# A twelve-stage decoder on one core: the second half of each norm's mean goes to the stage ahead, and the last context attention is entered by its keys with its ternary rounding cut into pieces

## The chip, the cores and the metric

The kernel runs on one core of a Trainium2 chip, written by hand for its five engines: PE (TensorE, matmuls), DVE (VectorE), ACT (ScalarE), POOL (GpSimd) and SP (SyncE, which issues the DMAs). The metric is the device time of one execution in microseconds.

## What is computed

The reference is a decoder of four layers over x of shape (2, 512, 256), with a context of (2, 1024, 256). Each layer has a self part, a context part and a feed-forward part, each added to x behind a norm:

```python
x = x + _L3_attn_ref(_layernorm(x, axis=-1), ...)
x = x + _L3_xattn_ref(_layernorm(x, axis=-1), ctx_1024, ctx_1024, L3_xattn_Wq, L3_xattn_bq, ...)
x = x + _L3_ffn_ref(_layernorm(x, axis=-1), L3_ffn_W1, L3_ffn_b1, L3_ffn_W2, L3_ffn_b2)

def _layernorm(x, axis=-1, eps=1e-05):
    m = jnp.mean(x, axis=axis, keepdims=True)
    v = jnp.var(x, axis=axis, keepdims=True)
    return (x - m) / jnp.sqrt(v + eps)
```

The last context attention (`L3_xattn`) is causal over 512 of the context's positions, with 16 heads of 64. The last feed-forward rounds both weight matrices to -1, 0 or 1: each matrix is divided by the mean of its absolute values, rounded and clipped.

## The kernel before

Activations lie transposed: 256 features on two groups of 128 partitions, 1024 tokens along the free axis. The tokens are two halves of 512, one for each batch entry; they are called half 0 and half 1. The residual `k.X` stays in SBUF throughout.

The program is twelve stages (`STAGES`, one for each part of a layer), and each writes the order of its five engines out by hand. Between two stages stands a fence (`Kernel.fence`, L178): PE, DVE, ACT and POOL drain, and all five engines wait until the four have. In the profiled execution the fences lie at 206.9, 271.8, 365.8, 443.9, 600.6, 653.9, 995.6, 1360.2, 1397.3, 1546.3 and 1848.9 us.

Each stage begins with a norm (class `Norm`, from L183), and each half of it is a chain over three engines: PE makes the mean by a matmul with a matrix of 1/256 (`mean`, L201), DVE subtracts it (`centre`, L207), ACT squares (`square`, L214), PE makes the variance (`var`, L220), ACT makes the inverse root with a Ln and an Exp (`root`, L227 and L229), and DVE multiplies (`scale`, L237). `ln` is the stage's own norm, and `nxt` the norm of the stage behind it. A stage can do the first steps of `nxt` for half 0 as soon as half 0 of the residual is done (`resid(1)`): with `nxt.early = 1` it does mean, centre and square; with 2 also variance, root and scale. Before the change six of the eleven stages have 2, and the stages that end at 600.6, 653.9, 1360.2, 1397.3 and 1546.3 have 1 (five); the stage that ends at 653.9 keeps it. What is left is done behind the fence by `open_tensor`, `open_scalar` and `open_vector`; `open_tensor` always makes the mean of half 1 first, and with `early` at 1 it issues five bf16 matmuls on the identity (`beat`, L157), whose results nobody reads, ahead of the variance.

The last context attention is `l3_xattn` (L2818). Its weights come in eight groups of two heads, G = 8. A group has eight units, a unit being 128 queries of one half with its 128 to 512 keys; N = 64. One loop over `step` is written for each engine, so that at step s PE makes the scores of unit s (L2886), DVE adds the causal mask and takes the maxima of unit s-1 (L3010), ACT takes its exponentials (L2970), DVE takes the reciprocals of unit s-2 (L3023), POOL scales with them (L3074), PE transposes the probabilities of unit s-3 (L2896), which ACT and DVE copy out (L2990, L3049), and PE multiplies unit s-7 with the values (L2932). `CHUNKS` places the projections: for each group q, k and v of both halves, six chunks, each made by PE at a step `at` (L2916, v at L2911) in one PSUM bank, `p_bank`, and copied out by DVE (q at L3032, v at L3038) or ACT (k at L2980). Each chunk waits until the one ahead of it is out of the bank. The first four, q0, k0, q1, k1, are made at steps -6, -5, -4 and -3, and PE waits for all four ahead of unit 0.

At steps 6 and 14 DVE and POOL round one weight matrix each of the last feed-forward (class `Ternary`, L2782): DVE sums 2048 absolute values per partition (L2792), POOL sums over the partitions (L2806), DVE makes scale and inverse (L2794, L2796) and then scales, rounds and clips the 2048 columns in three operations (L2798, L2800, L2802), all of it at one place in DVE's program.

## Time and profile before

| | |
|---|---|
| median of 3 runs | 1893.58 us (1891.5 to 1898.21) |
| profiled execution, device time | 1895.19 us |
| its span, first to last instruction | 1893.9 us |
| mean granted clock of TensorE | 0.961 |
| busy: PE, DVE, ACT, POOL | 89%, 56%, 48%, 23% of the span |
| stage of the last context attention | 1546.3 to 1848.9 us, 302.6 us |
| last stage (feed-forward) | from 1848.9 us |

Times in the rows further down are microseconds from the start of the span. A row of a timeline is start, duration, engine, line, operation, what it writes and reads, shape and count; in brackets the time for which its engine sat idle just before it, and what ended that. `DVEq L178` there is a fence. A granted clock of 1.00 is 2.4 GHz, 0.50 is 1.2 GHz.

### The profile page before, as it was taken

To read this page: it belongs to the slowest core of one execution; us is meant where nothing else is said; L and a number is where in the kernel's file an instruction comes from. 1 tells how busy PE (TensorE), PEld (TensorE's weight loads), DVE (VectorE), ACT (ScalarE), POOL (GpSimd) and SP (SyncE) were. 2 spreads that over 40 slices of the span, in tenths; PEclk is the share of its full clock that TensorE was granted. 3 is DMA by queue.
4 is the path that set the end of the run, shared out by engine and by line. 5 is a ranking of instruction groups with operands and counts; after the bars stand their busy time and mean duration, and the time that the engine had idled before them with its cause. 6 is when DMAs were issued, how large, how long until landed. Compare 5 with 4: busy or idle time off the path is not lost. (4 is left out here: it accounts for less than half of the span.)

```text
span 1893.9 us, 23001 instructions
## 1 busy us (share of the span) xinstructions
PE 1680.7 (89%) x7780; PEld 862.7 (46%) x7780; DVE 1053.0 (56%) x2140; ACT 905.3 (48%) x1762; POOL 428.8 (23%) x536
## 2 busy tenths in 40 slices
PE   7899996888998679999887899999888987899997
PEld 3334444334665234344334555655434433445545
DVE  4631125483313659888925788888448614555525
ACT  2331214352333247777823778887433732455523
POOL 0000000000000244555401455555201101223310
PEclk9999998999999999999998899999998987899999
DMA  5000100001000000000107111010127110000000
GB/s 214 1 0 0 39 1 1 34 1 45 1 1 17 1 9 18 9 9 9 48 1 240 55 59 39 30 35 26 57 53 217 39 72 10 13 18 21 1 0 23
DMA packets 31844, 69.42 MB, mean 37 GB/s; under 512 B 4213, under 2 KB 18357, under 8 KB 30293
## 3 DMA queue, kind: packets, MB, share of 16 engines
q1 hardware_dynamic: 31728, 67.95, 11.0%
q8 instruction: 63, 1.03, 0.2%
q14 instruction: 53, 0.43, 0.1%
HBM read 55.78 MB, written 12.06 MB: 36 GB/s over the span
## 5 line engine op out<-in xcount | busy, mean ns | idle before, releaser
L2247 POOL TENSOR_TENSOR work<-work,arena_a 128x512 f32<-128x512 f32 x128 | 167.6, 1310 | 151.7 <-ACT work L2112 151.5
L1986 PE MATMUL ps<-identity,ctx_keys 128*128 128x128 f32 x1024 | 145.0, 281 | 17.1 <-ACT work L2112 14.5
L2201 DVE CUSTOM_DVE_ANT_0 ctx_keys<-ps,arena_b 128x1024 f32<-128x1024 f32 x128 | 154.9, 1212 | 7.2 <-ACT arena_b L2063 7.0
L1986 PEld LDWEIGHTS ps<-identity,ctx_keys 128*128 128x128 f32 x1024 | 118.6, 144 | 64.9 <-ACT work L2112 21.3
L2094 ACT ACTIVATE ctx_keys<-ctx_keys,small 128x1024 f32<-128x1024 f32 x128 | 146.8, 1147 | 0.7 <-DVE small L2201 0.7
L2213 DVE TENSOR_TENSOR work<-ps,arena_a 128x512 f32<-128x512 f32 x128 | 88.0, 688 | 42.6 <-PE ps L1986 37.9
L3074 POOL TENSOR_SCALAR ctx_keys<-ctx_keys,small 128x128 f32<-128x128 f32 (+3 forms) x128 | 66.4, 531 | 199.3 <-DVE small L3023 185.3
L2112 ACT ACTIVATE work<-ps 128x512 f32<-128x512 f32 x128 | 76.3, 596 | 60.1 <-PE ps L1986 56.7
L338 PE MATMUL ps<-work,arena_a 128*128 128x512 f32 x192 | 86.8, 605 | 7.9 <-DVE work L512 3.2
L1788 POOL TENSOR_SCALAR work<-work 128x1024 f32<-128x1024 int32 x64 | 66.5, 1040 | 112.7 <-DVE work L1741 112.2
L2970 ACT ACTIVATE ctx_keys<-ctx_keys,small 128x128 f32<-128x128 f32 (+3 forms) x128 | 70.7, 554 | 41.0 <-DVE small L3010 40.5
L157 PE MATMUL ps<-identity 128*128 128x512 bf16 x340 | 82.4, 391 | 7.4 <-ACT work L1427 3.0
L1588 PE MATMUL ps<-work 64*128 64x512 f32 x256 | 73.2, 648 | 16.7 <-DVE work L1741 14.5
L1975 PE MATMUL ps<-work 96*128 96x512 bf16 x256 | 78.3, 388 | 10.6 <-DMA work<-parts_k_L_xattn 5.8
L201 PE MATMUL ps<-resid,mean_matrix 128*128 128x512 f32 x96 | 55.4, 707 | 35.0 <-DVEq L178 20.9
L1741 DVE SCALAR_TENSOR_TENSOR work<-work,ps 128x1024 int32<-128x1024 f32 x64 | 78.0, 1218 | 12.2 <-ACT work L1679 12.1
L214 ACT ACTIVATE norm_parts<-normed 128x1024 f32<-128x1024 f32 x24 | 25.2, 1051 | 124.1 <-DVE normed L207 124.1
L1724 DVE TENSOR_SCALAR work<-work,small 128x512 int16<-128x512 f32 x128 | 81.0, 674 | 2.3
L1663 ACT ACTIVATE work<-work 128x512 f32<-128x512 f32 x128 | 80.3, 643 | 2.4 <-POOL work L1788 2.4
L3049 DVE COPY work<-ps 128x128 f32<-128x128 f32 (+1 forms) x64 | 31.4, 491 | 84.9 <-PE ps L2896 84.3
L1155 POOL PARTITION_ALL_REDUCE small<-small x4 | 1.4, 358 | 338.7 <-DVE small L1151 338.7
L1612 PE MATMUL ps<-arena_a,work 128*64 128x512 f32 x256 | 66.3, 622 | 1.6 <-DVE work L1759 1.5
(387 smaller groups left out, 3451.4 us busy)
## 6 DMA issues: line engine op xcount, KB each, us to landing
arena_b<-in_mask SPq DMA_DIRECT2D x2, 2048.0 KB, 8.9
arena_a<-in_groupT SPq DMA_DIRECT2D x2, 2048.0 KB, 14.9
head_weights<-in_w_L_xattn SPq DMA_DIRECT2D x8, 449.0 KB, 3.3
arena_a<-in_w_l_attn SPq DMA_DIRECT2D x1, 3072.0 KB, 14.5
head_weights<-in_w_L_attn SPq DMA_DIRECT2D x8, 384.0 KB, 3.0
work<-parts_q_L_attn SPq DMA_DIRECT2D x8, 384.0 KB, 4.5
work<-parts_k_L_attn SPq DMA_DIRECT2D x8, 384.0 KB, 5.3
work<-parts_k_L_xattn SPq DMA_DIRECT2D x15, 192.0 KB
```

The lines of the kernel that those rows point to most:

```text
L157: self.pe.matmul(bank, ib[:, 0:P], ib.unsqueeze(1).broadcast_to([P, 2, 2 * P]), start=True, stop=True)
L338: mm = pe.matmul(k.bank(i), wT[:, c, m * P:(m + 1) * P], src[:, c, :], start=c == 0, stop=c == DC - 1)
L1663: op = act.activation(ex[i % NE][:, h, :], ex[i % NE][:, h, :], ACT.Exp, scale=1.0 / FX, accum_out=sums[i % 4][:, h:h + 1])
L1724: op = dve.tensor_scalar(attn[i % 2][:, h * S:(h + 1) * S], ex[i % NE][:, h, :], recip[i % 4][:, h:h + 1], OFFSET - HALF, OP.mult, OP.add)
L1741: dve.scalar_tensor_tensor(out=score[i % NS], in0=sign[i % 2], scalar=-HALF, in1=s_bank[i % 2], op0=OP.mult, op1=OP.add).then_inc(*truncat ...
L1975: mm = pe.matmul(s_psum[i % NS][:, o:o + S], qs[h][0:ROWS, q0:q0 + P], ks[h][0:ROWS, b * keys + o:b * keys + o + S], start=True, stop=True)
L1986: mm = pe.transpose(t_psum[z][:, kt * P:(kt + 1) * P], prob[i % NP][:, o:o + P], k.iden[:, :])
L2094: act.activation(p, p, ACT.Exp, scale=-1.0, bias=minmax[:, i % 8:i % 8 + 1], accum_out=sums[:, i % 8:i % 8 + 1]).then_inc(*exped.up())
L2112: act.activation(PT[i // 4 % 2][:, 4:8, i % 4 * P:(i % 4 + 1) * P], t_psum[1].rearrange("p (k t) -> p k t", t=P), ACT.Copy).then_inc(*turn ...
L2201: dve.tensor_tensor_reduce(prob[i % NP], s_psum[i % NS], NEG[:, b, qt, :], -1.0, BIG * 3e8, OP.add, OP.min, minmax[:, i % 8:i % 8 + 1]).th ...
L2213: dve.tensor_tensor(PT[i // 4 % 2][:, 0:4, qt * P:(qt + 1) * P], t_psum[0].rearrange("p (k t) -> p k t", t=P), GT[:, b, 0:4, qt * P:(qt + ...
L2247: pool.tensor_tensor(p, p, GT[:, b, 4:8, qt * P:(qt + 1) * P], OP.mult).then_inc(*weighed_pool.up())
```

## The change

1. In all eleven stages with a norm behind them, `nxt.second = True`, and PE makes the mean of half 1 for it at the end of the stage, behind `resid(2)`; `open_tensor` leaves it out.
2. At the fences at 600.6, 1360.2, 1397.3 and 1546.3 `nxt.early` goes from 1 to 2.
3. The last context attention makes its first chunks in the order k0, q0, k1, v0 at steps -6 to -3, and q1, v1 at steps 0 and 1. Chunks 1 and 3 (q0 and v0) use the bank `t_bank[0]`, so that there are two banks for the first chunks, and unit 0 waits for half 0 of q and k alone.
4. `Ternary` is gone. DVE sums the weights' absolute values in eight pieces of 512 columns, one at each of steps 3 to 10; PE sums them over the partitions with one small matmul at step 15 into `p_bank`; DVE makes both scales at step 16; and the rounding is 24 operations on 512 columns, one at each of steps 17 to 40.
5. On the host, the query and key weights of the second layer's context attention are no longer put in another order of columns. No instruction changes by this.

The diff, cut to its core (item 1 stands in the same form in the other stages):

```diff
@@ class Norm
         if self.early < 1:
             self.mean(pe, 0)
-        self.mean(pe, 1)
+        if not self.second:
+            self.mean(pe, 1)
         if self.early < 2:
             self.var(pe, 0, beats=5)
@@ l2_ffn
-        nxt.early = 1
+        nxt.early, nxt.second = 2, True
...
         leave(pe, 1)
+        if nxt:
+            nxt.var(pe, 0)
+            nxt.mean(pe, 1, resid(2))
...
             nxt.square(act, 0)
+            nxt.root(act, 0)
...
         add(1)
+        if nxt:
+            nxt.scale(dve, 0)
@@ l3_xattn
-    CHUNKS = [(0, what, n, at) for what, n, at in (("q", 0, -6), ("k", 0, -5), ("q", 1, -4), ("k", 1, -3))]
+    CHUNKS = [(0, what, n, at) for what, n, at in (("k", 0, -6), ("q", 0, -5), ("k", 1, -4), ("v", 0, -3), ("q", 1, 0),
+                                                   ("v", 1, 1))]
...
+    chunk_bank = lambda x: t_bank[0] if x in (1, 3) else p_bank
...
-                if i % per == 0:
-                    pe.wait_ge(*q_out(2 * g + 2))
-                    pe.wait_ge(*k_out(2 * g + 2))
+                if i % nk == 0:
+                    pe.wait_ge(*q_out(2 * g + b + 1))
+                    pe.wait_ge(*k_out(2 * g + b + 1))
...
-                if x:
+                ps = chunk_bank(x)
+                if x >= 4:
                     pe.wait_ge(*chunk_out(x - 1))
+                if 2 <= x <= 4:
+                    pe.wait_ge(*chunk_out(x - 2))
+                if step == 2 * per:
+                    pe.wait_ge(*ternary(9))
...
             if step == -5:
                 ln.var(pe, 1)
+            if step == 2 * per - 1:
+                pe.wait_ge(*ternary(8))
+                pe.wait_ge(*chunk_out(x))
+                pe.matmul(p_bank[:, 0:8], k.one[:, :], am, start=True, stop=True).then_inc(*magnitude.up())
...
-            if step in (6, 14):
-                j = int(step == 14)
-                if j:
-                    dve.wait_ge(*tern[0].done(6))
-                dve.wait_ge(*ffn_in(1))
-                tern[j].vector(dve, w_ffn[j], k.tern[:, 2048 * j:2048 * (j + 1)], k.extra[:, 0:2048])
+            round_weights(dve, step)
...
+    def round_weights(dve, step):
+        if step == 3:
+            dve.wait_ge(*ffn_in(1))
+        if 3 <= step < 11:
+            p = step - 3
+            dve.tensor_reduce(am[:, p:p + 1], k.WB[:, 2560 + S * p:2560 + S * p + S], AX.X, OP.add,
+                              apply_absolute_value=True).then_inc(*ternary.up())
+        if step == 2 * per:
+            dve.wait_ge(*magnitude(1))
+            dve.tensor_reduce(scale, p_bank[:, 0:8].rearrange("p (j c) -> p j c", j=2), AX.X, OP.add).then_inc(*ternary.up())
+            dve.wait_ge(*ternary(9))
+            dve.tensor_scalar(scale, scale, D / (P * 2048), 1e-8, OP.mult, OP.max).then_inc(*ternary.up())
+            dve.wait_ge(*ternary(10))
+            dve.reciprocal(inv, scale).then_inc(*ternary.up())
+        x = step - 2 * per - 1
+        if 0 <= x < 24:
+            p, op = divmod(x, 3)
+            part, src = tmp[:, piece(p % 4)], k.WB[:, 2560 + S * p:2560 + S * p + S]
+            dve.wait_ge(*ternary(11 + x))
+            if op == 0:
+                dve.tensor_scalar(part, src, inv[:, p // 4:p // 4 + 1], ROUND, OP.mult, OP.add).then_inc(*ternary.up())
+            elif op == 1:
+                dve.tensor_scalar(part, part, ROUND, 1.0, OP.subtract, OP.min).then_inc(*ternary.up())
+            else:
+                dve.tensor_scalar(tern[:, piece(p)], part, -1.0, None, OP.max).then_inc(*ternary.up())
```

## Rows read from the trace of the kernel before

**Rows 1.** The page: busy us (share of the span) and instructions, by engine.
```profile
PE 1680.7 (89%) x7780; PEld 862.7 (46%) x7780; DVE 1053.0 (56%) x2140; ACT 905.3 (48%) x1762; POOL 428.8 (23%) x536
```

**Rows 2.** Windows: stretch, length, busy us by engine, granted clock, DMA share, GB/s.
```profile
1546.31:1577.66 31.35, 22.80 (x33) 7.93 (x34) 5.38 (x8) 4.95 (x7) 0.00 (x0) 0.66 0.28 109
...
1577.66:1646.89 69.23, 53.44 (x258) 28.07 (x258) 38.71 (x112) 27.19 (x82) 14.98 (x31) 0.87 0.05 14
...
1608.26:1611.94 3.68, 3.68 (x12) 1.52 (x13) 1.58 (x6) 1.80 (x5) 2.00 (x4) 0.50 0.02 4
...
1644.37:1649.50 5.13, 5.13 (x19) 2.96 (x20) 2.31 (x10) 2.24 (x7) 1.99 (x4) 0.50 0.01 2
...
1675.52:1730.43 54.91, 54.91 (x307) 28.98 (x305) 28.02 (x105) 29.86 (x88) 16.61 (x33) 1.00 0.06 18
```

**Rows 3.** Timeline, fences at 271.8, 365.8, 443.9: start, us, instruction, [idle before].
```profile
267.32 1.22 DVE L671 TENSOR_TENSOR resid<-ps,resid 128x1024 f32<-128x1024 f32 x1 [5.58 <-PE ps L643]
...
270.41 1.29 DVE L237 TENSOR_TENSOR normed<-normed,norm_parts 128x512 f32<-128x512 f32 x2 [1.87 <-ACT norm_parts L229]
...
271.81 1.98 PE L201 MATMUL ps<-resid,mean_matrix 128*128 128x512 f32 x4 [2.81 <-DVEq L178]
...
273.93 1.29 DVE L207 TENSOR_TENSOR normed<-resid,ps 128x512 f32<-128x512 f32 x2 [2.22 <-PE ps L201]
...
363.31 1.23 DVE L896 TENSOR_TENSOR resid<-resid,work 128x1024 f32<-128x1024 f32 x1 [0.77 <-ACT work L825]
...
365.88 3.63 PE L201 MATMUL ps<-resid,mean_matrix 128*128 128x512 f32 x4 [3.62 <-DVEq L178]
...
443.97 3.22 PE L201 MATMUL ps<-resid,mean_matrix 128*128 128x512 f32 x4 [2.82 <-DVEq L178]
```

**Rows 4.** Timeline, PE and DVE around the fences at 1360.2 and 1397.3.
```profile
1359.40 0.75 DVE L2228 SCALAR_TENSOR_TENSOR resid<-ps,vecs,resid 128x512 f32<-128x512 f32 x1 [0.97 <-PE ps L2042]
...
1367.97 1.96 PE L2290 MATMUL ps<-normed,arena_b 128*128 128x512 f32 x4 [2.94 <-DVE normed L237]
...
1405.04 3.67 PE L2514 MATMUL ps<-normed,extra 128*128 128x512 f32 x8 [2.94 <-DVE normed L237]
```

**Rows 5.** Timeline, ACT and DVE around the fences at 600.6 and 653.9.
```profile
598.23 1.05 ACT L214 ACTIVATE norm_parts<-normed 128x1024 f32<-128x1024 f32 x1
...
614.30 1.22 DVE L1439 TENSOR_REDUCE small<-normed 128x1 f32<-128x1024 f32 x1
...
652.80 1.06 ACT L214 ACTIVATE norm_parts<-normed 128x1024 f32<-128x1024 f32 x1 [22.32 <-DVE normed L207]
```

**Rows 6.** Timeline, PE at the entry of the last context attention.
```profile
1546.36 3.78 PE L201 MATMUL ps<-resid,mean_matrix 128*128 128x512 f32 x4 [0.89 <-DVEq L178]
...
1556.12 2.57 PE L2916 MATMUL ps<-normed,head_weights 128*128 128x512 f32 x4 [2.94 <-DVE normed L237]
...
1568.35 3.75 PE L2916 MATMUL ps<-normed,head_weights 128*128 128x512 f32 x4 [2.81 <-issue]
...
1577.66 0.80 PE L2886 MATMUL ps<-work 64*128 64x128 f32 x4 [0.87 <-ACT work L2980]
```

**Rows 7.** Timeline, the two ternary roundings: DVE, POOL and PE.
```profile
1596.72 2.28 DVE L2792 TENSOR_REDUCE small<-arena_b 128x1 f32<-128x2048 f32 x1
...
1607.49 1.62 POOL L3074 TENSOR_SCALAR ctx_keys<-ctx_keys,small 128x128 f32<-128x128 f32 x4 [7.03 <-issue]
...
1608.26 0.69 PE L2896 MATMUL ps<-identity,ctx_keys 128*128 128x128 f32 x2 [8.09 <-POOL ctx_keys L3074]
...
1644.37 0.69 PE L2896 MATMUL ps<-identity,ctx_keys 128*128 128x128 f32 x2 [6.95 <-POOL ctx_keys L3074]
```

**Rows 8.** Timeline, a 512-wide cast, and the tight unit (21) of the attention.
```profile
1861.94 0.43 DVE L3173 CAST parts<-arena_a 128x512 fp32r<-128x512 f32 x1 [0.63 <-ACT arena_a L3149]
...
1674.63 0.93 POOL L3074 TENSOR_SCALAR ctx_keys<-ctx_keys,small 128x256 f32<-128x256 f32 x2 [3.86 <-DVE small L3023]
...
1675.94 0.66 PE L2896 MATMUL ps<-identity,ctx_keys 128*128 128x128 f32 x4
```

More of the change, by code:

```diff
@@ L190, in __init__ @@
         self.w, self.b, self.put, self.spare = w, b, put, spare
-        self.shared, self.early = sq[0] is sq[1], 0
+        self.shared, self.early, self.second = sq[0] is sq[1], 0, False
         self.mean_done, self.var_done = k.signals("pe", 2)
@@ L315, in l0_attn @@
     if nxt:
-        nxt.early = 2
+        nxt.early, nxt.second = 2, True
     bank = lambda *i: [k.bank(j) for j in i]
@@ L610, in l0_xattn @@
     if nxt:
-        nxt.early = 2
+        nxt.early, nxt.second = 2, True
     scored, mixed = k.signals("pe", 2)
@@ L650, in tensor @@
                         nxt.var(pe, 0)
+                        nxt.mean(pe, 1, resid(2))
     def scalar(act):
@@ L713, in l0_ffn @@
     if nxt:
-        nxt.early = 2
+        nxt.early, nxt.second = 2, True
     l0_ffn_loads(k, k.sp)
@@ L779, in tensor @@
             nxt.var(pe, 0)
+            nxt.mean(pe, 1, resid(2))
     def mix(pe, h):
@@ L935, in l1_attn @@
     if nxt:
-        nxt.early = 2
+        nxt.early, nxt.second = 2, True
     l1_attn_loads(k, k.sp)
@@ L980, in tensor @@
             nxt.var(pe, 0)
+            nxt.mean(pe, 1, resid(2))
     def scalar(act):
@@ L1197, in l1_xattn @@
     if nxt:
-        nxt.early = 1
+        nxt.early, nxt.second = 2, True
     l1_xattn_loads(k, k.sp)
@@ L1272, in tensor @@
                 nxt.mean(pe, 0, resid(1))
+        if nxt:
+            nxt.var(pe, 0)
+            nxt.mean(pe, 1, resid(2))
     def scalar(act):
@@ L1351, in vector @@
         close(dve, 1)
+        if nxt:
+            nxt.scale(dve, 0)
     def close(dve, b):
@@ L1383, in l1_ffn @@
     if nxt:
-        nxt.early = 1
+        nxt.early, nxt.second = 1, True
     in_q, hid_q = Quantizer(k, view(k.small, 8, 4)), Quantizer(k, view(k.small, 12, 4))
@@ L1418, in tensor @@
             nxt.mean(pe, 0, resid(1))
+            nxt.mean(pe, 1, resid(2))
     def scalar(act):
@@ L1554, in l2_attn @@
     if nxt:
-        nxt.early = 2
+        nxt.early, nxt.second = 2, True
     l2_attn_loads(k, k.sp)
@@ L1651, in tensor @@
                         nxt.var(pe, 0)
+                        nxt.mean(pe, 1, resid(2))
     def scalar(act):
@@ L1872, in l2_xattn @@
     if nxt:
-        nxt.early = 1
+        nxt.early, nxt.second = 2, True
     thin_loads(k, k.sp, name)
@@ L2027, in tensor @@
         close(pe, 1)
+        if nxt:
+            nxt.var(pe, 0)
+            nxt.mean(pe, 1, resid(2))
     def turn_back(pe, n):
@@ L2118, in scalar @@
             nxt.square(act, 0)
+            nxt.root(act, 0)
     def gather(act, n):
@@ L2223, in vector @@
         absorb(dve, 1)
+        if nxt:
+            nxt.scale(dve, 0)
     def absorb(dve, n):
@@ L2276, in l2_ffn @@
     if nxt:
-        nxt.early = 1
+        nxt.early, nxt.second = 2, True
     l2_ffn_loads(k, k.sp)
@@ L2333, in tensor @@
         leave(pe, 1)
+        if nxt:
+            nxt.var(pe, 0)
+            nxt.mean(pe, 1, resid(2))
     def scalar(act):
@@ L2360, in scalar @@
             nxt.square(act, 0)
+            nxt.root(act, 0)
     def vector(dve):
@@ L2385, in vector @@
         add(1)
+        if nxt:
+            nxt.scale(dve, 0)
     sync(k.sp)
@@ L2443, in l3_attn @@
     if nxt:
-        nxt.early = 1
+        nxt.early, nxt.second = 2, True
     l3_attn_loads(k, k.sp)
@@ L2571, in tensor @@
             project(pe, m, (A_BANK[2], k.bank(3))[m], 1, (3,)).then_inc(*final.up())
+        if nxt:
+            nxt.var(pe, 0)
+            nxt.mean(pe, 1, resid(2))
     def transposed(pe, u, late):
@@ L2657, in scalar @@
             nxt.square(act, 0)
+            nxt.root(act, 0)
     def gather(act, v):
@@ L2731, in vector @@
         absorb(dve, 1)
+        if nxt:
+            nxt.scale(dve, 0)
     def finish(dve, x):
@@ L2827, in l3_xattn @@
     causal, wo, oT = view(k.WB, 0, S), view(k.WB, S, G, D), view(k.WA, 0, G, NT)
-    w_ffn = [k.WB[:, 2560 + 2048 * j:2560 + 2048 * (j + 1)] for j in range(2)]
     NP = 4
@@ L2840, in l3_xattn @@
     n_keys = lambda i: (i % nk + 1) * P
-    CHUNKS = [(0, what, n, at) for what, n, at in (("q", 0, -6), ("k", 0, -5), ("q", 1, -4), ("k", 1, -3))]
+    CHUNKS = [(0, what, n, at) for what, n, at in (("k", 0, -6), ("q", 0, -5), ("k", 1, -4), ("v", 0, -3), ("q", 1, 0),
+                                                   ("v", 1, 1))]
     for g in range(G):
-        CHUNKS += [(g, "v", n, per * g + n) for n in range(B)]
+        if g:
+            CHUNKS += [(g, "v", n, per * g + n) for n in range(B)]
         if g + 1 < G:
@@ L2851, in l3_xattn @@
     if nxt:
-        nxt.early = 2
+        nxt.early, nxt.second = 2, True
     l3_xattn_loads(k, k.sp)
     w_in = k.ahead["l3_xattn"]
-    tern = [Ternary(k, view(k.small, 200 + 4 * j, 4)) for j in range(2)]
+    tern, tmp, piece = k.tern, k.extra[:, 0:2048], lambda p: slice(S * p, S * p + S)
+    am, scale, inv = (view(k.small, o, n) for o, n in ((200, 8), (208, 2), (210, 2)))
     consts_in, ffn_in = k.signals("dma", 2)
-    part, scored, turn, pv, final = k.signals("pe", 5)
+    part, scored, turn, pv, final, magnitude = k.signals("pe", 6)
     k_out, exped, turned_0, gathered = k.signals("act", 4)
-    q_out, v_out, maxed, inverse, turned_1, resid = k.signals("dve", 6)
+    q_out, v_out, maxed, inverse, turned_1, resid, ternary = k.signals("dve", 7)
     (weighed,) = k.signals("pool", 1)
+    chunk_bank = lambda x: t_bank[0] if x in (1, 3) else p_bank
     chunk_out = lambda x: {"q": q_out, "k": k_out, "v": v_out}[CHUNKS[x][1]](2 * CHUNKS[x][0] + CHUNKS[x][2] + 1)
@@ L2915, in tensor @@
                     for c in range(DC):
-                        mm = pe.matmul(p_bank, W[g % 2][what == "k"][:, c, :], src[:, c, t0:t0 + S], start=c == 0,
+                        mm = pe.matmul(ps, W[g % 2][what == "k"][:, c, :], src[:, c, t0:t0 + S], start=c == 0,
                                        stop=c == 1)
@@ L2953, in close @@
                     nxt.var(pe, 0)
+                    nxt.mean(pe, 1, resid(2))
     def scalar(act):
@@ L2979, in scalar @@
                         act.wait_ge(*scored(per * (g - 1)))
-                    act.activation(kT[g % 2][:, half(n)], p_bank, ACT.Identity,
+                    act.activation(kT[g % 2][:, half(n)], chunk_bank(x), ACT.Identity,
                                    bias=weights[g % 2][:, 897:898]).then_inc(*k_out.up())
@@ L3031, in vector @@
                         dve.wait_ge(*scored(per * (g - 1)))
-                    dve.tensor_scalar(q[s][:, half(n)], p_bank, weights[s][:, 896:897], 0.125, OP.add,
+                    dve.tensor_scalar(q[s][:, half(n)], chunk_bank(x), weights[s][:, 896:897], 0.125, OP.add,
                                       OP.mult).then_inc(*q_out.up())
@@ L3066, in gpsimd @@
         for step in range(N + 2):
-            if step in (6, 14):
-                tern[int(step == 14)].gpsimd(pool)
             i = step - 2
@@ L3316, in lay_out @@
             ws, bs = list(ws), list(bs)
-            for j in range(2):
+            for j in range(2 if n == "L3_attn" else 0):
                 ws[j] = ws[j].reshape(D, DC, 8, 16).transpose(0, 1, 3, 2).reshape(D, D)
```

25 lines of the change are left out of this document (2 added, 23 removed).

## The prediction

> **What bounds the kernel now.** I read in this order. The page's busy times: TensorE (PE) is busy 89% of the span, the next engine 56% [rows 1]; so an edit is worth what it takes off PE's waits or off its time at half clock, and DVE, ACT and POOL matter where PE waits for them. Windows over the last context attention (1546 to 1849 us): from the fence to the first score PE has a granted clock of 0.66 and takes 31.35 us over 22.80 us of work; the next 16 units take 69.23 us at 0.87, while 16 units in the middle take 54.91 us, PE busy in all of it, at 1.00 [rows 2]. So this stage is PE-bound except at its entry and in its first 16 units. The timelines show why. Twice PE waits for POOL, 8.09 and 6.95 us, and behind each wait the clock is 0.50 [rows 2, 7]. At the entry the small groups of PE work alternate with DVE and ACT [rows 6]. Last the timelines at the other fences: behind every one PE makes the mean of half 1 first, 1.98 us at full and up to 3.78 us at half clock, and DVE's subtraction waits for it [rows 3, 6].
>
> **Part 1, the mean of half 1 ahead of the fence (11 fences).** It needs the second residual half, so it can't come earlier than that plus its own time. What it gains depends on what else sets the fence.
>
> Where DVE scales half 0 behind the residual, the scaling covers it. At 271.8 the residual ends at 268.54 and the scaling (1.29 us) starts only at 270.41 [rows 3]; PE sits idle for the last 2.81 us before the fence, from 269.0, so mean 1 runs to 271.0 and the fence stays. PE's first work then moves from 273.7 to 271.85, DVE's subtraction from 273.93 to 271.85: gain 2.1. Three more are of this kind. At 443.9 the same cover holds and the mean removed cost 3.22 us, partly at half clock [rows 3]: 3.3. At 365.8 it cost 3.63 [rows 3], but the residual ends only 1.3 us before the fence, so 2 us of mean move the fence by 0.7, by 2.4 if they fall at half clock: gain between 1.2 and 2.9, 2.2 taken. At 995.6 the residual is as late: the fence moves by 0.7, PE gains 2.0 behind it, and the stage goes on with transfers through memory that start 0.7 later (SP's mask and group loads stand behind the fence too): -0.7 to +1.3, I take 0.7. At 1848.9 it is hidden, but nothing waits for it behind the fence, since DVE splits half 0 first: 0. At 206.9 no scaling is left behind the residual, mean 1 only changes sides: -0.1. At 653.9 the fence is set by ACT's square, which ends at 653.86 [rows 5], and mean 1 ends at 653.2: the fence stays and what follows comes 1.8 earlier.
>
> **Part 2, early 1 to 2 (behind four fences).** Variance 0, its root and the scaling of half 0 go ahead of the fence, and five filler matmuls go. At 1360.2: PE ends its projection at 1359.4, where DVE's last residual starts [rows 4], variance 0 to 1361.2, root 0.69 + 0.63, scaling 1.29 (row of the same kind in [rows 3]): fence at 1364.0 in place of 1360.2, mean 1 hidden under the root. L2290 starts there, at 1364.05 in place of 1367.97 [rows 4]. Half 1 gains a little less, since its variance now stands directly behind L2290: 3.4. The next fence (1397.3) has the same order, but variance 0 and mean 1 overlap ACT and residual better: L2514 from 1405.04 [rows 4] to 1401.3, 3.7; SP's three loads and POOL's memsets start 4 us later there, and their first reader is later still. At 600.6: square 0 ends at 599.3 [rows 5], so the fence is at 604.0; subtraction, square, variance, root, scaling of half 1 lead to the second maximum at 611.2 in place of 614.30 [rows 5]: 3.1 at full clock, 1.4 if the variance falls at half clock because its fillers are gone; 2.0 taken. Sum of the ten fences: 2.1 + 3.3 + 2.2 + 0.7 + 0 - 0.1 + 1.8 + 3.4 + 3.7 + 2.0 = 19.1 us, between 9 and 24.
>
> **Part 3, the entry of the last context attention.** Now: fence 1546.3, mean 3.78, fillers, variance, root, scaling, q0 at 1556.12, wait, k0 1559.62, variance 1, wait for the scaling, q1 1568.35, wait, k1 1573.04, wait, first score 1577.66 [rows 6]. After: the last projection ends 0.89 us before PE's mean [rows 6], at 1545.4, variance 0 takes 1.9 to 3.6, root 1.4, scaling 1.3: fence between 1550.0 and 1552.5, I take 1551. Then k0, q0, variance 1, k1, v0 need nothing that PE has to wait for: k0 no norm at all, q0 half 0, and two banks take turns, so an eviction (0.75 us) runs under the next chunk. Variance 1 needs subtraction and square, ready 2.4 us behind the fence; PE gets to it after 3.7. Five groups of 1.88 to 1.98 us are 9.5 us at full clock, at half (3.75 us per chunk [rows 6]) 17. Since PE is then dense from that projection on, but for about a microsecond before the fence, I take full clock but for 1 us: first score at 1561.5, gain 16.1; bounds 8 and 18. The chunk q1 moves behind the first score and takes the place there that v0 had: no cost. The causal mask must land before unit 0 and the weights before the first sum; both were issued behind the fence and need 3 and 10 us, under the 10 us of chunks and the steps that follow.
>
> **Part 4, the ternary rounding.** Removed, twice: a sum of 2048 (2.28 us), POOL's sum over partitions (0.40), two small operations and three of 2048 (1.29 + 1.23 + 1.23) in one piece on DVE, while TTR and reciprocals of the attention queue behind it. POOL comes back to its scalings only 7.03 us after that sum [rows 7], longer than DVE's part explains. PE's waits are 8.09 + 6.95 = 15.0 us; the half clock behind them (3.68 and 5.13 us at 0.50 [rows 2]) costs half of 8.8, 4.4. Together 19.4. Added: eight sums of 512 on DVE in steps 3 to 10, 24 operations of 512 in steps 17 to 40 (0.43 us each, by the row of a 512-wide cast [rows 8]; the sums by a quarter of 2.28, 0.57), one tiny matmul in step 15, and in step 16 a wait of PE's v chunk for DVE's sum over its result. Behind that wait stand PE's mix of that step and the next score; DVE does the sum right behind unit 15's maxima, near the time PE gets there: at most 0.5. The pieces stand on DVE between the maxima and the reciprocal, so a unit's scaling on POOL comes 0.43 later. Seven of eight units have 2 to 5 us between POOL's end and PE's transposes; the tight one is every eighth: POOL ends at 1675.57, PE starts 1675.94 [rows 8], slack 0.38. Three or four such units lose 0.1 to 0.5 each. Taken off: 1.0. Net 18.4, between 12 (clock gains nothing, every piece shows a little) and 19.4.
>
> A piece on DVE with one SBUF source may also hold up POOL. The rows don't decide it: POOL's next scaling starts at 1607.49 [rows 7], behind DVE's three large operations, where it lacked its reciprocal anyway. The Trainium skill ("SBUF — State Buffer", "SBUF: two separate sides") says more: such a DVE operation and a GpSimd operation take a shared port pair for a whole instruction, and the other fully blocks. By it each piece could add another 0.43 us to POOL's part; beside the sum above that would be some 2 us more.
>
> **Sum.** 19.1 + 16.1 + 18.4 = 53.6 us. Against the profiled execution's 1895.2 us: 1841.6; the median of the runs is 1.6 lower, which gives 1840. I forecast 1841.
>
> **Rivals.**
> (a) *Half clock stays at the places made dense.* For: clock 0.66 over the entry now [rows 2], and the fillers are gone behind four fences. Against: waits of 2.8 us before a mean left it at 1.98 us [rows 3]. Entry gain 8 to 10, fences 3 to 5 less: about 1853. The Trainium skill ("TensorE: Matmul & The Clock Gate", "Part 1: The HAM clock gate (the "warmup" mystery)") says that throttled is the default and that sustained matmul activity releases it. By that rule the dense entry would end at full clock, nearer to my forecast.
> (b) *The mean only changes sides.* If every fence moves by what is saved behind it, as at 206.9, the 19.1 fall away: 1860. Against: the cover at 271.8 and 653.9 is in the rows [rows 3, 5].
> (c) *The pieces show.* If each of the 32 pieces holds PE for 0.43 to 0.86 us, 14 to 27 us of the rounding's gain come back: about 1861. Against: slack of 2 to 5 us in seven of eight units.
> (d) *Slower than before.* Place: units 17 to 40, where the 24 pieces stand. If waits for late transposes break up PE's work so often that it runs at half clock, a unit of 54.91 / 16 = 3.43 us takes 6.9. It decides from 16 such units on (16 x 3.43 = 55 us, more than the sum); all 24 give 1841 + 82 = 1923. Against: 1.00 and no gap now, and a piece of an eighth of a unit.
> (e) *More than the sum.* Waits that I put at one place also ended at others, and the clock gains in stages that I count as shifted only: 1829.
> That the change doesn't do what it says (some other transfer or bank holds the entry) is a case of (a) by price.
>
> **How the numbers follow.** Forecast (1832 to 1848) 0.66, (a) 0.14, (b) 0.05, (c) 0.06, (d) 0.02, (e) 0.07. The range takes forecast and (a), 1832 to 1855. A difference of 0.3% (5.7 us) is about what can be told from none. All but (d) and a small rest lie beyond it on the fast side: faster 0.96, within 0.3% 0.02, slower 0.02.
>
> **What would show it.** Part 1 and 2: behind each fence no L201 on PE, DVE's subtraction at once, and the fence-to-fence lengths shorter by the terms above. Part 3: five groups without a gap and a first score 10 to 12 us behind the fence. Part 4: no PE wait over 1 us in units 5 to 16, 16 units from the first score in some 50 us, and period 27.5 us per eight units unchanged. It is wrong if PE's busy time in units 17 to 40 has gaps, if the granted clock at the entry stays near 0.5, or if stage lengths elsewhere stay as they are.

## The result and the profile after

The changed kernel takes 1847.3 us (median of 4 runs, 1846.75 to 1848.24), the kernel before beside it 1892.54 us (4 runs). The ratio is 0.9758, with a 95% interval from 0.9734 to 0.9781. The forecast was 1841 with a range of 1832 to 1855: the sign and the range hold, and the sum of the gains was 6 us too large. The profiled execution took 1846.75 us (span 1845.4), 48.4 us less than that of before.

The page of the changed kernel, busy times by engine; PE is busy 21.9 us less than in [rows 1]:

```profile
PE 1658.8 (90%) x7762; PEld 854.0 (46%) x7762; DVE 1052.5 (57%) x2163; ACT 905.1 (49%) x1762; POOL 428.8 (23%) x534
```

Windows of the changed kernel (columns as in [rows 2]): from the fence to the first score, 16 units, 16 units with rounding pieces in them, and the whole stage of the last context attention, from fence to fence:

```profile
1539.97:1548.87 8.90, 8.84 (x32) 4.90 (x32) 3.33 (x5) 3.63 (x5) 0.00 (x0) 1.00 0.88 353
1548.87:1599.88 51.01, 49.06 (x250) 24.88 (x249) 30.90 (x107) 26.06 (x80) 14.12 (x28) 1.00 0.08 24
1599.88:1654.85 54.97, 54.97 (x306) 28.97 (x304) 32.95 (x121) 29.73 (x88) 16.46 (x32) 1.00 0.06 18
1539.97:1800.78 260.81, 255.81 (x1298) 132.01 (x1298) 132.64 (x463) 124.25 (x358) 66.85 (x128) 1.00 0.07 25
```

The entry fell from 31.35 to 8.90 us, the next 16 units from 69.23 to 51.01, all at full clock, and 16 units with 15 of the 24 rounding pieces among them take 54.97 us with PE busy throughout, where 16 quiet ones took 54.91 [rows 2]. Over the whole stage the clock is 1.00. The timeline of PE at that entry (columns as in [rows 6]):

```profile
1535.33 1.88 PE L220 MATMUL ps<-norm_parts,mean_matrix 128*128 128x512 f32 x4
1537.05 1.88 PE L201 MATMUL ps<-resid,mean_matrix 128*128 128x512 f32 x4
1540.03 1.98 PE L2929 MATMUL ps<-ctx_feat,head_weights 128*128 128x512 f32 x4 [1.10 <-DVEq L178]
1541.85 1.88 PE L2929 MATMUL ps<-normed,head_weights 128*128 128x512 f32 x4
1543.57 1.88 PE L220 MATMUL ps<-norm_parts,mean_matrix 128*128 128x512 f32 x4
1545.28 1.88 PE L2929 MATMUL ps<-ctx_feat,head_weights 128*128 128x512 f32 x4
1547.00 1.95 PE L2924 MATMUL ps<-head_weights,ctx_feat 128*128 128x128 f32 x16
1548.88 0.49 PE L2894 MATMUL ps<-work 64*128 64x128 f32 x4
```

Variance 0 and mean 1 stand ahead of the fence; behind it come k0, q0, variance 1, k1 and v0 without a gap.

Where the 48.4 us are: 41.8 in the stage of the last context attention (302.56 to 260.81, fence to fence), 6.3 in the ten stages ahead of it, 0.3 in the last. The forecast had 39.2 in that stage and 14.4 ahead of it: its 53.6, where the later fence (4.7 us at 1546.3) counts against the ten stages and for the entry.

### The profile page after: what moved, and what is told of

It is laid out like the page before. It is cut to its first block and busy times, and to the rows that moved or that the text cites. A ratio compares the mean times of both kernels' runs of the same rounds, so it can differ in the third digit from the quotient of the medians.

```text
span 1845.4 us, 22986 instructions
## 1 busy us (share of the span) xinstructions
PE 1658.8 (90%) x7762; PEld 854.0 (46%) x7762; DVE 1052.5 (57%) x2163; ACT 905.1 (49%) x1762; POOL 428.8 (23%) x534
## 5 line engine op out<-in xcount | busy, mean ns | idle before, releaser
L1989 PE MATMUL ps<-work 96*128 96x512 bf16 x256 | 79.3, 393 | 14.2 <-DMA work<-parts_k_L_xattn 9.4
L1647 PE MATMUL ps<-normed,head_weights 128*128 128x512 f32 x128 | 63.7, 620 | 3.8 <-DVE work L1746 3.0
## 6 DMA issues: line engine op xcount, KB each, us to landing
arena_a<-in_groupT SPq DMA_DIRECT2D x2, 2048.0 KB, 14.8
```

The costliest lines, as they stand in the source:

```text
L1989: mm = pe.matmul(s_psum[i % NS][:, o:o + S], qs[h][0:ROWS, q0:q0 + P], ks[h][0:ROWS, b * keys + o:b * keys + o + S], start=True, stop=True)
```

## The experiments

All times are medians; "before" is the kernel before, run on the same chip alongside (1892.98 to 1896.05 us there).

**One half of the change at a time.** `norm_moves_only` has items 1 and 2 of the change and leaves items 3 and 4 out.

> All eleven norm moves (the mean of half 1 at every fence, the variance at four), with the last context attention's chunks and its rounding as before. Theory S (the sum as forecast): the ten other fences give 19.1 us, and at the fence of 1546.3 mean, fillers, variance, root and scaling (about 8 us) leave the entry, of which the order q0, k0, q1, k1 keeps its waits: 27 us faster than before. Theory T (transfers started by the fence set the pace of the second layer's and the last layer's attention, so the gains at 995.6, 1397.3 and part of 653.9 are given back there): the ten fences give 9, and the whole 15 to 18 us. Under T the gain counted up to the fence of 1546.3 is 8 to 10 us, under S 19.

Measured: 1876.58 us (1872.96 to 1877.35), before 1892.98; ratio 0.9896 (0.9860 to 0.9931). That is 16.4 us, T's value and not S's 27, though the interval reaches from 13 to 27. S's 27 was also added up wrongly: it takes the 8 us off the entry in full, while the forecast itself has 4.7 of such work come back ahead of the fence at 1546.3, which leaves 22. T's size doesn't prove T's places: by the means in the table further down, 0.4 us are given back behind 653.9, 0.6 behind 995.6 and 3.4 behind 1397.3. In this profile the first score comes 16.71 us behind the fence, with q1 at half clock (3.48 us).

`last_attention_only` has items 3 and 4 and leaves the norms as they were.

> Only the last context attention is changed (keys first, two banks, rounding in pieces); all norms as before. Stages ahead of it keep their lengths within 1 us. Forecast: rounding 18.4 us, and from the entry what the order of the chunks gives without the earlier variance, about 8: 26 us faster. Theory T with norm_moves_only: the gains of the two kernels add up to the 45.3 us of the whole change within 3 us. Rival C (the clock makes the two help each other, since half 1's chunks come at full clock only if the norm's gap is gone too): the two add up to less than 42.

Measured: 1862.19 us (1858.31 to 1869.78), 30.8 less than before; ratio 0.9832 (0.9784 to 0.9881). More than the forecast's 26. 16.4 and 30.8 make 47.2, and the whole change gave 45.2 on one chip and 49.6 on another: they add up, and nothing speaks for C.

`pieces_only` has item 4 alone.

> Only the ternary rounding is cut into pieces; norms and the order of the first chunks as before. Forecast: 18.4 us faster than before (12 to 19.4), no PE wait over 1 us in units 5 to 16, the entry as long as before. Rival (the rounding's gain as read in the changed kernel was partly the entry's, by its clock): 12 us or less.

Measured: 1871.73 us (1864.33 to 1880.3, 7 runs), before 1896.05; ratio 0.9890 (0.9853 to 0.9928), 14 to 28 us. The rival's 12 us or less is out. PE has no wait over 0.8 us behind the first score, and from there to the last fence of the stage it takes 251.3 us, against 271.2 before. But the entry, whose code is that of before, took 25.27 us and not 31.35, at a granted clock of 0.90 and not 0.66. That was expected by neither theory.

`keys_first_only` has item 3 alone; of its edit, the order of the chunks:

```diff
-    CHUNKS = ... (("q", 0, -6), ("k", 0, -5), ("q", 1, -4), ("k", 1, -3))
+    CHUNKS = ... (("k", 0, -6), ("q", 0, -5), ("k", 1, -4), ("v", 0, -3), ("q", 1, 0), ("v", 1, 1))
```

> The kernel before with only the order of the first chunks and the second bank; norms and rounding as before. The norm chain behind the fence stays, and k0 runs under it. Forecast from the rows of before: q1 (3.75 us), k1's wait and two evictions leave the path to the first score, some 8 to 12 us; the two waits of the roundings (15.0 us) stay. last_attention_only was 30.8 us faster than before and pieces_only 20 to 24, which also leaves 7 to 11 for this part. Rival (the second bank helps only when the norm is there already): 4 us or less.

Measured: 1885.83 us (10 runs), before 1894.12; ratio 0.9945 (0.9923 to 0.9967), 6 to 15 us. The first score comes 14.88 us behind the fence, and PE's two waits at the roundings are there (7.75 and 7.34 us). The median's 8.3 us is at the low end of the forecast's 8 to 12, and the rival's 4 or less is out. With `pieces_only` it makes 32.6 us by medians, against 30.8.

**Is the half clock at the old entry the rule?** `before_again` and `after_again` are the two kernels unchanged, for second profiles.

> The kernel before once more, for a second profile of it. In pieces_only, whose entry to the last context attention is that of the kernel before, the first score came 25.27 us behind the fence at full clock, not 31.35 as in the profile that the forecast read. Theory V (the half clock at that entry comes and goes from one execution to the next, and the profiled execution had all of it): this profile shows the first score at 25 to 28 us, a stage of 296 to 300 us in place of 302.6, and the roundings' two waits unchanged. Rival (the entry at half clock is the rule, and pieces_only was the exception): 31 us and 302 us again. Ratio of times 1.

Measured: 1894.36 us, ratio 1.0027 (0.9999 to 1.0056). Windows of this second profile of before (fence to first score, next 16 units), and its timeline at the entry:

```profile
1548.93:1574.20 25.27, 16.73 (x33) 6.16 (x34) 5.37 (x8) 4.95 (x7) 0.00 (x0) 0.90 0.34 136
1574.20:1642.02 67.82, 52.72 (x259) 27.46 (x259) 38.70 (x112) 27.20 (x82) 14.99 (x31) 0.88 0.05 14
```

```profile
1548.98 3.78 PE L201 MATMUL ps<-resid,mean_matrix 128*128 128x512 f32 x4 [0.89 <-DVEq L178]
...
1559.11 1.96 PE L2916 MATMUL ps<-normed,head_weights 128*128 128x512 f32 x4 [2.94 <-DVE normed L237]
...
1568.48 1.96 PE L2916 MATMUL ps<-normed,head_weights 128*128 128x512 f32 x4 [2.81 <-issue]
...
1574.20 0.49 PE L2886 MATMUL ps<-work 64*128 64x128 f32 x4 [0.87 <-ACT work L2980]
```

The waits are those of [rows 6] (2.94, 2.81, 0.87), but q1 takes 1.96 us and not 3.75. The stage takes 295.75 us instead of 302.56. V holds: the 6 us of half clock at that entry come and go between executions (of three profiles with this entry, one has 31.35 us and two have 25.27), while the two rounding waits stay (7.83 and 6.52 us). The shorter entry is not at full clock throughout, as V's text has it of `pieces_only`: the mean ahead of it still takes 3.78 us, and the granted clock is 0.90. What decides between the two isn't shown.

> The changed kernel once more, on the same chip as before_again. First score 8.90 us behind the fence and a stage of 260.8 us again; the nine stages ahead of it add up to 1540 to 1543 us (1539.97 in its first profile). Theory V: the difference of the two kernels' times stays 45 us; that of the stage of the last context attention is 36 to 39 us by these two profiles, not 41.8 as by the first two.

Measured: 1844.74 us (1843.96 to 1850.62), before 1894.25; ratio 0.9757 (0.9712 to 0.9803). The first score again at 8.90 us and the stage at 260.80; the ten stages ahead took 1537.67 us, a little under the span expected. By the two new profiles the stage gained 34.95 us, just under V's 36 to 39, and the stages ahead of it 11.3. The medians on this chip differ by 49.5 us, not by 45.

**What of the rounding costs?** `rounding_in_two_bursts` is the changed kernel, with the 24 operations made six:

```diff
-        x = step - 2 * per - 1
-        if 0 <= x < 24:
-            p, op = divmod(x, 3)
...
+        if step in (2 * per + 1, 3 * per + 1):
+            j = int(step == 3 * per + 1)
+            src, dst = k.WB[:, 2560 + 2048 * j:4608 + 2048 * j], tern[:, 2048 * j:2048 * (j + 1)]
...
```

> The changed kernel, but the 24 rounding operations of 512 columns are six of 2048, three in a row at step 17 and three at step 25; sums and PE's sum over partitions stay in pieces. Forecast's reading of the waits removed (DVE's three long operations in one piece, 3.75 us, hold the maxima and reciprocals of the units behind them): each burst holds PE for 3 to 5 us, 6 to 10 us slower than the changed kernel, with PE waiting for POOL's scaling twice. Rival (the waits before came from POOL's own sum over the partitions, after which POOL came back only 7.0 us later): within 2 us of the changed kernel.

Measured: 1850.14 us (1848.72 to 1851.75), before 1894.12, ratio 0.9764 (0.9732 to 0.9796); the stage takes 264.18 us instead of 260.8. Timeline of this kernel, DVE, POOL and PE at the first burst:

```profile
1602.29 1.28 DVE L3091 TENSOR_SCALAR extra<-arena_b,small 128x2048 f32<-128x2048 f32 x1
...
1603.61 1.23 DVE L3093 TENSOR_SCALAR extra<-extra 128x2048 f32<-128x2048 f32 x1
...
1604.87 1.23 DVE L3095 TENSOR_SCALAR ternary_weights<-extra 128x2048 fp32r<-128x2048 f32 x1
...
1606.01 0.16 DVE L3036 RECIPROCAL small<-small 128x2 f32<-128x2 f32 x1
...
1606.26 1.36 POOL L3111 TENSOR_SCALAR ctx_keys<-ctx_keys,small 128x512 f32<-128x512 f32 x2 [3.78 <-DVE small L3036]
...
1606.90 2.02 PE L2924 MATMUL ps<-head_weights,ctx_feat 128*128 128x128 f32 x16 [1.60 <-DVE work L3051]
```

The same three long operations that stood ahead of the 8.09 us wait in [rows 7] now cost PE 1.60 us, and 1.39 at the second burst, not for POOL but for a copy of DVE. So cutting the three long operations is worth 3.4 us, by the stage, of the 18.6 to 19.3 that the whole rounding gave; the medians (1850.14 against 1844.74 to 1849.85 for the changed kernel and near relatives) can't tell so little. Both texts were off in size: the forecast's reading (6 to 10) by more than the rival's. The other 15 us or so hang on what is common to this kernel and the changed one: POOL's sum over partitions gone to PE, DVE's sum of 2048 cut and moved ahead, and the operations at steps 17 and 25 instead of 6 and 14. These were not separated by a run. The rows of before allow an estimate for the first wait of 8.09 us. DVE is held there from 1596.72 [rows 7] to 1604.61, 7.89 us, of which 1.49 is its own wait for POOL's sum; that is 4.2 more than the 3.72 of the burst, which cost PE 1.60. And POOL starts its scaling 2.7 us after the reciprocal that it needs (1604.77 to 1607.49), where in the burst it starts 0.1 after it. If PE pays for both in full, 1.6 + 4.2 + 2.7 make 8.5, near the 8.09:

```profile
1600.49 0.15 DVE L2794 TENSOR_SCALAR small<-small 128x1 f32<-128x1 f32 x1 [1.49 <-POOL small L2806]
...
1604.61 0.16 DVE L3023 RECIPROCAL small<-small 128x2 f32<-128x2 f32 x1
```

**Where the fences' gain goes.** `one_variance_undone` is the changed kernel with the variance of half 0 taken back at one fence, 1397.3 (stage `l2_ffn`):

```diff
-        nxt.early, nxt.second = 2, True
+        nxt.early, nxt.second = 1, True
...
-            nxt.var(pe, 0)
...
-            nxt.root(act, 0)
...
-            nxt.scale(dve, 0)
```

> The changed kernel with the variance, root and scaling of half 0 back behind the fence at 1397.3 (early 1, five filler matmuls again; the mean of half 1 stays ahead). Forecast: 3.7 less 1.9 for the mean that stays, so 1.8 to 2 us slower than the changed kernel. Theory T (all that the earlier fence gave is taken back by the transfers of the last layer's attention): within 1 us of it, or up to 2 us faster, since the three loads then have time to land ahead of the stores.

Measured: 1848.02 us (1840.98 to 1850.83) against 1847.3, 1848.28 and 1844.74 for the changed kernel and near relatives on three chips: the time doesn't decide. The profile shows more, by DVE's position in the stage behind, `l3_attn`, counted from the fence ahead of `l2_ffn`. There DVE comes to a place where it waits for PE's next score. Its last instruction ahead of that wait starts at 84.59 us, against 78.85 in the changed kernel: the earlier variance brings 5.7 us there. The first behind it starts at 86.70 against 85.61: 1.1 are left. In the kernel before the two start at 89.22 and 90.33, so against it 10.4 us become 4.7. The wait, in the changed kernel and with the variance taken back:

```profile
1442.23 0.42 DVE L2748 CUSTOM_DVE_ANT_0 arena_b<-ps,arena_b 128x256 f32<-128x256 f32 x1 [6.69 <-PE ps L2560]
```

```profile
1439.79 0.42 DVE L2744 CUSTOM_DVE_ANT_0 arena_b<-ps,arena_b 128x256 f32<-128x256 f32 x1 [2.04 <-PE ps L2556]
```

What is left at the fence that ends `l3_attn` can't be read so finely: it comes at 186.6 us, and with the variance in place, the code of these two stages being the same, at 182.8 to 185.8 in six profiles. T is right on the place; whether it is right on "all" stays open. The timeline of SP shows what lies between. First the changed kernel, its fence at 1390.98:

```profile
1391.01 0.32 SPq L2488 DMA_DIRECT2D work<-in_alibi_q  x1
1391.37 0.35 SPq L2489 DMA_DIRECT2D work<-in_alibi_k  x1
1391.77 0.27 SPq L2490 DMA_DIRECT2D work<-in_alibi_one  x1
1397.49 1.59 SPq L2497 DMA_DIRECT2D parts_q_L_attn<-arena_a  x3
...
1408.55 0.33 SPq L2521 DMA_DIRECT2D work<-parts_q_L_attn  x1
```

Then the kernel before, its fence at 1397.27:

```profile
1397.30 0.32 SPq L2462 DMA_DIRECT2D work<-in_alibi_q  x1
...
1411.45 1.59 SPq L2471 DMA_DIRECT2D parts_q_L_attn<-arena_a  x3
...
1419.17 0.33 SPq L2495 DMA_DIRECT2D work<-parts_q_L_attn  x1
```

The first stores are issued 6.5 us behind the fence and not 14.2, but their read-back, which waits for them to land, only 11.06 us after them and not 7.72. In the changed kernel the stores run into the three loads that the fence starts. With the variance taken back the distance is 7.83 again (1399.71 to 1407.54). That is 3.3 of the 7.7 us by which the stores are earlier. More goes in the later round trips of the same kind: the fourth read-back is issued 38.8 us behind the fence where it was 42.0, only 3.1 us earlier. The reader sees the end of it on PE, in the changed kernel:

```profile
1440.84 0.93 PE L2614 MATMUL ps<-work 111*128 111x512 bf16 x2 [6.36 <-DMA work<-small]
```

`alibi_later` moves these loads:

```diff
     def sync(sp):
-        sp.dma_start(qs[0:BIAS], a["alibi_q"].bitcast(BF16)).then_inc(*const_in.up())
...
+            if x == 1:
+                sp.dma_start(qs[0:BIAS], a["alibi_q"].bitcast(BF16)).then_inc(*const_in.up())
...
```

> The changed kernel with one edit: in the last layer's attention SP issues its three loads of the position table (alibi) behind the first two stores of the cut-up activations, not ahead of them. In the changed kernel the first of these stores lands 4.7 us after its issue (2.6 before), and PE waits 6.4 us for the pieces that come back. Theory T (that queue sets the pace, and the loads stand in front of it): the wait shrinks to what it was before the change and the kernel is 2 to 5 us faster than the changed one. Forecast's reading (the loads cost nothing there): within 1 us of it.

Measured: 1851.65 us (1849.69 to 1854.66), not faster. The transfers that T named do hold up the first round trip, for the distance from store to read-back falls to 6.63 us. But the cure is wrong: PE now waits for one of the loads ahead of the first score, and the later wait that was to shrink is still there (6.70 us, 6.36 in the changed kernel). The timelines of SP and PE in this kernel, and from the view of the tile that the loads and the read-back write, the time from issue to landing, which it has for the two read-backs (4.2 to 5.0 us in the changed kernel):

```profile
1399.50 1.59 SPq L2494 DMA_DIRECT2D parts_q_L_attn<-arena_a  x3
...
1406.13 0.32 SPq L2522 DMA_DIRECT2D work<-parts_q_L_attn  x1
```

```profile
1419.88 4.04 PE L157 MATMUL ps<-identity 128*128 128x512 bf16 x12 [3.11 <-DMA work<-in_alibi_one]
```

```profile
DMA to landing us min/median/max: 11.8/13.3/14.8
```

The stage takes 155.1 us against 149.0. `group_load_later` makes the same attempt in `l2_xattn` (the stage from 995.6; it is layer L2's, which the expectation calls the second):

```diff
-        fields(0)
+        sp.dma_start(NEG[:, 0].bitcast(I32), mask[0]).then_inc(*mask_in[0].up())
         for x in range(3):
             store(sp, x)
+        sp.dma_start(GT[:, 0], group[0]).then_inc(*group_in[0].up())
```

> The changed kernel with one edit in the second layer's context attention: SP issues the load of the first half of groupT behind the first three stores, not ahead of them. Theory T: in the changed kernel the three stores are issued 6.6 us behind the fence (8.6 before) and their first read-back 17.6 us behind it (17.1 before), because the 4 MB of mask and group are in the queue; with the group behind them the read-back is issued 2 to 5 us earlier and the kernel is 2 to 3 us faster. Rival (as alibi_later showed for the last layer: what is taken from in front of a store comes back behind it): the read-back is earlier, but a later transfer takes it back; within 1 us of the changed kernel.

Measured: 1848.28 us (1845.79 to 1851.48), ratio 0.9755. The rival is right: the read-back is issued 13.65 us behind the fence (999.81, fence at 986.16) instead of 17.6, and the stage still takes 371.6 us.

`mean_995_undone` takes back the mean of half 1 at the fence at 995.6 (`second` off and `nxt.mean(pe, 1, resid(2))` out, in that stage only).

> The changed kernel with the mean of half 1 back behind the fence at 995.6 alone. Forecast: 0.7 us slower than the changed kernel. Theory T: PE's mean hides under the transfers that the fence starts, and the fence comes 0.7 to 1 us earlier, so the kernel is 0 to 4 us faster, 4 if all of the 4.1 us by which that stage is longer in the changed kernel than in the one before (369.4 against 365.3 us, means of four and three profiles) hang on it.

Measured: 1849.85 us (1841.15 to 1854.63), ratio 0.9757; the stage behind takes 372.0 us, not 365. So the longer stage doesn't hang on the mean. The comparison in my expectation was wrong as well: the fence at 1360.2 that ends the stage is 3.6 us later by design (below), so the stage had to grow.

`four_variances_undone` takes back the variance, root and scaling of half 0 at all four fences of item 2.

> The changed kernel with the variance, root and scaling of half 0 back behind the fences at 600.6, 1360.2, 1397.3 and 1546.3 (early 1, with the five filler matmuls); the means of half 1 stay ahead. Forecast: the variance's share there, 2.0 + 1.5 + 1.8 us, and at the last entry the first score 14.9 less 3.8 for the mean, 11 us behind a fence that is 2 to 3 us earlier, so about 0 there: 5 us slower than the changed kernel. Theory T (the 1.8 at 1397.3 are lost to transfers anyway): 3 us slower.

Measured: 1856.27 us (1854.66 to 1859.79) against 1844.74 for `after_again` on the same chip: 11.5 us slower, more than twice both expectations. In the profiles 1.7 of it lie behind 600.6, 3.2 in `l2_xattn` and `l2_ffn` together, 3.0 in `l3_attn` and 4.3 in the last context attention, where the first score comes 13.21 us behind the fence and not 11. The 3.0 in `l3_attn` is no more than the same code differs by from one profile to the next (148.4 to 151.4 us in four profiles with the new norms). My expectations gave back the whole delay of a fence with the variance. But the mean of half 1 stays ahead of it, and the scaling that covered it is gone: in `one_variance_undone` the distance from PE's last own matmul to the fence fell from 5.5 to 3.54 us only, where it was 1.5 before the change, and here it is 2.9 at 1360.2 and 1546.3, where it was 0.84. At these fences the mean is free ahead of the fence only together with the scaling; the two parts of the change belong together.

## Why the prediction was right, and where its sum was off

The stage lengths, from fence to fence in us. The forecast's column follows from its terms: what is saved behind the first fence, and by how much the second fence moves. "Pair" is the difference of the two first profiles, "mean" that of five profiles with the old norms (both of before and three experiments) and four with the new ones (both of the changed kernel, `norm_moves_only` and `rounding_in_two_bursts`).

| stage ends at (before) | forecast | pair | mean | spread of the five |
|---|---|---|---|---|
| 206.9 | +2.0 | +0.5 | +1.2 | 2.0 |
| 271.8 | -1.9 | -1.4 | -1.6 | 0.0 |
| 365.8 | -1.4 | -1.3 | -0.4 | 6.1 |
| 443.9 | -2.9 | -4.7 | -3.7 | 1.2 |
| 600.6 | +0.1 | +0.1 | +0.1 | 0.0 |
| 653.9 | -5.4 | -3.8 | -5.0 | 0.9 |
| 995.6 | -1.1 | +0.7 | -0.7 | 6.0 |
| 1360.2 | +2.4 | +6.4 | +3.0 | 6.1 |
| 1397.3 | -3.2 | -2.7 | -3.7 | 1.7 |
| 1546.3 | -3.0 | -0.1 | +0.4 | 2.8 |
| sum | -14.4 | -6.3 | -10.5 | |

**Parts 1 and 2, fences.** The mechanism was right. From PE's last matmul of the stage's own work to the fence it takes the same 4.48 us at 271.8 and 443.9, with the mean in it (the cover that the forecast named), and 2.04 us more at 206.9, 0.82 at 995.6, 3.48 at 600.6, 3.64 at 1360.2, 4.0 at 1397.3: forecast 2.0, 0.7, 3.4, 3.8, 4.0. At 365.8 it takes 1.5 us more (1.8 in `after_again`), where 0.7 was forecast. Rows of the changed kernel at 271.8 [rows 3]: mean 1 runs under the end of the stage, DVE subtracts at once.

```profile
267.91 1.88 PE L201 MATMUL ps<-resid,mean_matrix 128*128 128x512 f32 x4
...
269.49 1.29 DVE L237 TENSOR_TENSOR normed<-normed,norm_parts 128x512 f32<-128x512 f32 x2 [1.87 <-ACT norm_parts L229]
...
271.02 1.28 DVE L207 TENSOR_TENSOR normed<-resid,ps 128x512 f32<-128x512 f32 x2 [0.24 <-DVEq L178]
```

With the 3.6 us by which the fence at 1546.3 moved (4.7 in the forecast), the ten fences brought 10 us in the pair and 14 in the mean, not 19.1. The step that failed is the clause on 1397.3, "SP's three loads and POOL's memsets start 4 us later there, and their first reader is later still": the first reader is not who waits. The loads stand in the queue ahead of the round trip through memory that sets that stage's pace. That stage falls short by 3.4 us, of the 3.9 by which the mean of the ten stages falls short of the forecast's 14.4; the spread of that stage is nearly as large, 2.8. Most of the rest of the pair's shortfall lies in stages where the same code differs by 6 us from one profile to the next (last column), and I don't explain it.

**Part 3, the entry.** Right in mechanism: five dense groups at full clock, the first score 8.90 us behind the fence (10.5 forecast). In the pair the entry gained 22.45 - 3.64 = 18.8 us, more than the 16.1. But the term's base was one execution's half clock. Against `before_again` it is 25.27 - 8.90 - 3.64 = 12.7. So 6 us of the forecast's base were half clock that the kernel before does not always have, and that the pair reached the 16.1 was luck; the forecast's median, taken as 1.6 below the profiled execution, could not allow for it.

Rival (a) said that half clock would stay at the places made dense. At the entry it didn't: 1.00 in all windows above. By the rule of the Trainium skill cited there ("TensorE: Matmul & The Clock Gate", "Part 1: The HAM clock gate (the "warmup" mystery)"), that sustained matmul activity releases the throttle, the dense entry should be at full clock; the trace agrees. Behind three of the four fences whose fillers are gone the clock is 1.00 over 15 us as well. Behind the one at 600.6 it is 0.86 (0.89 before), and the variance of half 1 takes 2.74 us there, 3.75 in `after_again`: that is the half clock which the forecast's part 2 allowed for at this fence.

**Part 4, the rounding.** 18.4 us forecast. From the first score to the end of the stage it is 271.2 and 270.5 us in the two profiles of before, 251.9 in both of after: 19.3 and 18.6. Each piece took 0.42 to 0.48 us (0.43 forecast), the sums 0.68 and not 0.57, and both hid: the 1.0 us taken off for the tight units was not needed. Groups of DVE in the changed kernel, 1600 to 1700 us (line, operation, count, busy us, mean ns, idle before):

```profile
L3093 DVE TENSOR_SCALAR extra<-arena_b,small 128x512 f32<-128x512 f32 x8 | 3.9, 482 | 0.0
L3095 DVE TENSOR_SCALAR extra<-extra 128x512 f32<-128x512 f32 x8 | 3.4, 426 | 0.0
L3097 DVE TENSOR_SCALAR ternary_weights<-extra 128x512 fp32r<-128x512 f32 x8 | 3.4, 423 | 0.0
```

Rivals (c) and (d) are out by the window of 54.97 us at 1.00 and by the whole stage at 1.00, in which PE has no wait over 0.8 us behind the first score. The term is right in size, but the forecast's first reading of its cause, the long operations on DVE, was the smaller part: two bursts of the same three operations cost 3.4 us. By the estimate above the larger part lies with DVE's sum, POOL's sum and the waits of both engines around it; no run separates them, and the forecast had left that half open with POOL's return only 7.03 us after its sum.

A piece on DVE can hold up POOL, a little. POOL's scalings of 384 columns, in the stretch with the pieces (1540 to 1700 us, first row) and behind it:

```profile
L3113 POOL TENSOR_SCALAR ctx_keys<-ctx_keys,small 128x384 f32<-128x384 f32 x22 | 13.1, 608 | 20.4 <-DVE small L3036 20.4
```

```profile
L3113 POOL TENSOR_SCALAR ctx_keys<-ctx_keys,small 128x384 f32<-128x384 f32 x10 | 5.7, 585 | 5.4 <-DVE small L3036 5.4
```

The 23 ns more in the mean are two of the 128 scalings, the only ones that overlap a rounding piece from its start to its end; they took 0.82 and 0.85 us, not 0.59, and the same two did in `after_again`. All other scalings have the same length with and without pieces. The rule cited from the Trainium skill ("SBUF — State Buffer", "SBUF: two separate sides") is that one of two such operations shuts the other out for its whole length. The page ties this to VectorE operations in a mode that uses two ports or with two SBUF inputs, not to every one with a single source. The trace agrees in part: both scalings grew, but by 0.24 and 0.27 us, less than a piece. The 2 us estimated from the rule did not show, since the other 22 pieces overlap a scaling by 0.19 us at most.

**Rival (b)** (the mean only changes sides) is refuted at 271.8, 443.9 and 653.9, where the fence is as far behind PE's last own matmul as before. The sum's error has two sources, then: 3.4 us of transfers, and 3.4 (16.1 - 12.7) of an entry priced at a half clock that is there in some executions only. In the pair itself the split is another: the ten fences gave 9 us less than forecast, and the entry 2.7 and the rounding 0.9 more.

## What to carry to other kernels

Work moved ahead of a fence is free where another engine's last step already covers it, and that could be read from the rows to 0.2 us at nine of the eleven fences here (not at 365.8 and 1546.3). What it gives behind the fence is kept only where the next stage is not waiting for a memory round trip: list what the fence starts on the DMA queue, and ask whether the stores that are now earlier still run behind it. And before a stall is priced at half clock, look at a second profile of the same kernel.

## What was not expected of the hardware

The same code entered the last context attention in 31.35 us in one execution and 25.27 in another, q1's group taking 3.75 or 1.96 us, with equal waits ahead of it. Stores issued 7.7 us earlier behind a fence had their read-back only 4.3 us earlier, while three loads were in flight; with the loads behind the stores instead, the two read-backs took 11.8 and 14.8 us to land. A scaling of 128x384 on POOL took 0.82 to 0.85 us instead of 0.59 when a DVE operation of 128x512 ran from its start on.
